# A sort's opening in a graph-network kernel: digit staircases from the integers, both image halves ahead of the columns, all tiles normalised on ScalarE

## The reference

```python
h = jnp.maximum(_layernorm(x, axis=-1), 0.0)                  # x: 1024 x 512
h = (h - mean_over_nodes) * rsqrt(var_over_nodes + EPS) * bn_w + bn_b
# graph convolution over 16384 edges (src, dst) and 1024 loops
deg = segment_sum(ones, dst);  norm = deg[src]**-0.5 * deg[dst]**-0.5
h = segment_sum((h @ W)[src] * norm[:, None], dst) + b
for i in range(4):      # four layers: attention against cond, then a gated feed-forward
    ...
h = graph_convolution(h) ; return x + h + x_in
```

## Time and profile before

| | us |
|---|---|
| median of 3 runs | 2408.67 (2406.61 to 2410.69) |
| the profiled execution, its own time | 2408.46 |
| its span, first to last instruction | 2406.7 |
| mean granted TensorE clock | 0.994 |

### The profile page before, as it was taken

One profiled execution on the slowest core, in us unless ns is written; L12 is line 12 of the kernel. 1 busy time (PEld: TensorE's weight loads), 2 busy tenths in 40 slices (PEclk: granted clock), 3 DMA queues, 4 the chain that ended last, 5 costly groups with the idle time before them and its releaser, 6 DMA issues.

```text
span 2406.7 us, 32703 instructions
## 1 busy us (share of the span) xinstructions
PE 2357.1 (98%) x11951; PEld 1956.0 (81%) x11951; DVE 1651.5 (69%) x3177; ACT 1119.3 (47%) x2206; POOL 669.1 (28%) x439
## 2 busy tenths in 40 slices
PE   6899999999999999999999999999999999999999
PEld 4358888888888888878888888878888888888887
DVE  9986767775566767775666767775566766775554
ACT  9954444644334444644334444644334444554332
POOL 3111000066540000066540000066540000066540
PEclk9999999999999999999999999999999999999999
DMA  2031000122211100122211110122211100122222
GB/s 79 19 127 40 36 33 21 36 69 76 66 58 36 36 34 20 36 69 76 67 57 36 36 35 19 36 64 77 65 62 36 36 21 33 36 66 75 67 102 86
DMA packets 83306, 124.99 MB, mean 52 GB/s; under 512 B 5904, under 2 KB 63888, under 8 KB 78288
## 3 DMA queue, kind: packets, MB, share of 16 engines
q1 hardware_dynamic: 82864, 118.75, 14.9%
q10 hardware_dynamic: 288, 4.19, 0.4%
HBM read 116.36 MB, written 6.55 MB: 51 GB/s over the span
## 4 chain that ended last, share of the span: by engine, by line
PE 88%; DVE 8%; ACT 3%; issue 1%; POOL 0%; DMA 0%; SPq 0%; DVEq 0%; ACTq 0%; POOLq 0%
PE ps L2026 19%; PE ps L2028 19%; PE ps L2027 19%; PE ps L2365 7%; PE ps L2369 7%; PE ps L2367 6%; PE ps L2273 2%; PE ps L2290 2%; PE ps L2292 2%; DVE oh_d L1504 1%; PE ps L2287 1%; PE ps L2563 1%; DVE w_lo L1889 1%; DVE z L1884 1%; ACT z L1024 1%
## 5 line engine op out<-in xcount | busy, mean ns | idle before, releaser
L623 POOL TENSOR_TENSOR rstd<-veps,mhalf 128x1 f32<-128x1 f32 x48 | 28.9, 602 | 892.9 <-DVE veps L1294 892.9
L724 POOL TENSOR_TENSOR f_lo<-ff,f_hi 128x512 fp32r<-128x512 f32 x128 | 167.0, 1315 | 165.4 <-ACT f_hi L1183 165.3
L1957 DVE TENSOR_TENSOR h<-h,ps 128x512 f32<-128x512 f32 x256 | 168.9, 684 | 63.1 <-PE ps L2028 62.5
L975 ACT ACTIVATE v_hi<-ps 128x512 fp32r<-128x512 f32 x128 | 76.8, 600 | 285.0 <-PE ps L2028 285.0
L2026 PE MATMUL ps<-cond_hi,w_hi 128*128 128x512 f32 x512 | 202.1, 395 | 0.0
L2026 PE MATMUL ps<-wf_hi,f_hi 128*128 128x512 f32 x512 | 199.6, 390 | 2.0 <-DVE ff L1941 2.0
L2026 PE MATMUL ps<-w_hi,cond_hi 128*128 128x512 f32 x512 | 200.8, 392 | 0.0
L2028 PE MATMUL ps<-w_hi,cond_lo 128*128 128x512 f32 x512 | 200.3, 391 | 0.0
L2027 PE MATMUL ps<-cond_lo,w_hi 128*128 128x512 f32 x512 | 200.1, 391 | 0.0
L2028 PE MATMUL ps<-cond_hi,w_lo 128*128 128x512 f32 x512 | 200.1, 391 | 0.0
L2027 PE MATMUL ps<-w_lo,cond_hi 128*128 128x512 f32 x512 | 199.9, 390 | 0.0
(11 more groups left out here) (327 smaller groups left out, 6430.3 us busy)
## 6 DMA issues: line engine op xcount, KB each, us to landing
stage<-in_pieces SPq DMA_DIRECT2D x82, 512.0 KB, 3.3
stage<-in_condT SPq DMA_DIRECT2D x31, 1024.0 KB, 4.8
stage<-in_pieces SPq DMA_DIRECT2D x224, 128.0 KB, 2.6
at_s<-at_hi ACTq DMA_DIRECT2D x2, 2048.0 KB, 8.2
at_hi<-at_s SPq DMA_DIRECT2D x4, 1024.0 KB, 6.5
x<-in_x SPq DMA_DIRECT2D x2, 1024.0 KB, 6.9
out<-h SPq DMA_DIRECT2D x8, 256.0 KB, 2.0
bias_row<-in_rows SPq DMA_DIRECT2D x6, 256.0 KB, 3.9
```

Source lines behind the costliest of these rows:

```text
L724: pool.tensor_tensor(f_lo[q % 2][:, c, half * HALF:(half + 1) * HALF], ff[:, s % 2, :], bits(f_hi[q % 2][:, c, half * HALF:(half + 1) * HA ...
L1957: dve.tensor_tensor(h[:, t, :], h[:, t, :], ps[:, down_bank(q, t), :], ALU.add)\
```

## The change

Line numbers of the code after are given as such. The change touches the opening only.

- Digit staircases. ScalarE's 32 signs read the integer destination `ends_i` with steps of 32 in place of the shifted, converted digit. VectorE makes the first 9 itself, as 0 or 2, right ahead of `x_stats_of(0)`; ScalarE makes 8 at its start, 9 after `need_row`, 6 after the first eight column signs. The shift and half of the cast are gone, and one small instruction is added ahead of `deg`.
- `x_stats_of(1)` moves on VectorE from behind the positions to before them; `z1` of tiles 4 to 7 moves from VectorE to ScalarE; TensorE transposes all eight tiles before column 0; `pos` and `chunk_up` stand in bank 3 instead of 7.
- `d_low` on GpSimd is split in halves, one ahead of the normalisation constants and one behind.
- On ScalarE `w_high` of both pieces moves from before `z1` to behind the signs and digits; on GpSimd `w_low` moves with it.
- On VectorE the scatters 8 to 15 move from before `batch_scale` to behind it; on ScalarE signs 8 to 15 move from before `y` to behind it. The block of products on TensorE moves from column 15 to column 7, and each later product four columns earlier.

The numbers and places:

```diff
-    G_AT = {G_FIRST + 1 + 9 * n // 2: one for n, one in enumerate(G_GROUPS)}
+    G_AT = {G_FIRST - 3 + 9 * n // 2: one for n, one in enumerate(G_GROUPS)}
-        pos, chunk_up = ps[:, 7, 0:CHUNKS], ps[:, 7, CHUNKS:2 * CHUNKS]
+        pos, chunk_up = ps[:, 3, 0:CHUNKS], ps[:, 3, CHUNKS:2 * CHUNKS]
```

On GpSimd:

```diff
+            d_low_of(0)
             for half in range(2):
...
-                if half == 0:
-                    w_low(0, 0, attn_place(0, 0, 0), attn_place(1, 0, 0))
+            d_low_of(1)
+            w_low(0, 0, attn_place(0, 0, 0), attn_place(1, 0, 0))
             pool.wait_ge(b_ln, 2 * KC)
```

On ScalarE:

```diff
+            act.wait_ge(ends_in, 32)
+            act.wait_ge(steps_ok, 1)
+            d_apart(APART_BY_VECTOR, APART_BY_VECTOR + 8)
             act.wait_ge(col_mm, 1)
...
-            for n in range(2):
-                w_high(n, n, attn_place(0, 0, n))
             for t in range(4):
                 z1_of(t)
+            for t in range(4):
+                x0T_of(t)
+            for t in range(4, NT):
+                z1_of(t)
+            for t in range(4, NT):
+                x0T_of(t)
             act.wait_ge(iota_ok, 1)
             act.wait_ge(pos_ok, 4)
             signs(0, 8)
-            for t in range(4):
-                x0T_of(t)
-            for t in range(4, NT):
-                x0T_of(t)
-            d_apart(18, 32)
-            signs(8, G_FIRST + 1)
+            d_apart(26, 32)
+            for n in range(2):
+                w_high(n, n, attn_place(0, 0, n))
             for k in range(KC):
```

On VectorE:

```diff
+            for v in range(APART_BY_VECTOR):
+                last = dve.tensor_scalar(d_high[:, v, :], ends_i[:, 1, :], 32.0 * v, 2.0, ALU.is_ge, ALU.mult)
...
             x_stats_of(0)
+            x_stats_of(1)
...
-            x_stats_of(1)
+            batch_stats(0)
+            low_equal()
+            batch_stats(1)
             dve.wait_ge(pay_ok, 3)
             dve.wait_ge(pos_ok, 5)
             scatters(0, 8)
-            for t in range(4, NT):
-                z1_by_vector(t)
-            low_equal()
-            batch_stats(0)
-            batch_stats(1)
-            scatters(8, G_FIRST + 1)
             batch_scale()
             for k in range(2):
                 y_of(k)
+            scatters(8, 10)
...
+            scatters(10, 13)
             y_low(2)
...
+            scatters(13, G_FIRST + 1)
             y_low(3)
```

On TensorE:

```diff
-                if c == G_FIRST:
+                if c == 7:
                     pe.wait_ge(w_ok, 1)
```

More of the change, by code:

```diff
@@ L610, in _ @@
                       allow_small_or_imprecise_dtypes=True).then_inc(iota_ok, 1)
-            pool.iota(steps[:, :], pattern=[[-2, 32]], base=1, channel_multiplier=0,
+            pool.iota(steps[:, :], pattern=[[-64, 32]], base=1, channel_multiplier=0,
                       allow_small_or_imprecise_dtypes=True).then_inc(steps_ok, 1)
@@ L632, in _, with d_low_of @@
             pool.wait_ge(iota_ok, 1)
-            pool.tensor_tensor(d_low[:, :, :], d5[:, 0, :].unsqueeze(2).broadcast_to([P, CHUNKS, 32]),
-                               iota0[:, 0:32].unsqueeze(1).broadcast_to([P, CHUNKS, 32]),
-                               ALU.subtract).then_inc(d_low_ok, 1)
+            def d_low_of(which):
+                r, n = slice(which * CHUNKS // 2, (which + 1) * CHUNKS // 2), CHUNKS // 2
+                pool.tensor_tensor(d_low[:, r, :], d5[:, r].unsqueeze(2).broadcast_to([P, n, 32]),
+                                   iota0[:, 0:32].unsqueeze(1).broadcast_to([P, n, 32]),
+                                   ALU.subtract).then_inc(d_low_ok, 1)
+            d_low_of(0)
             for half in range(2):
@@ L802, in cond_high, with d_apart @@
                                ACT.Copy).then_inc(c_hi, 1)
+            def d_apart(first, end):
+                for v in range(first, end):
+                    last = act.activation(d_high[:, v, :], ends_i[:, 1, :], ACT.Sign, scale=2.0, bias=steps[:, v:v + 1])
+                last.then_inc(d_apart_ok, 1)
+            act.wait_ge(ends_in, 32)
+            act.wait_ge(steps_ok, 1)
+            d_apart(APART_BY_VECTOR, APART_BY_VECTOR + 8)
             act.wait_ge(col_mm, 1)
@@ L820, in _ @@
                 .then_inc(need_ok, 1)
[L822 to L829, removed]
+            d_apart(APART_BY_VECTOR + 8, 26)
             def z1_of(t):
-                act.wait_ge(x_rs, 4)
+                act.wait_ge(x_rs, 4 + t // 4 * 4)
                 act.activation(z1[:, t, :], x1[:, t, :], ACT.Identity, scale=x_rstd[:, t:t + 1],
@@ L885, in _ @@
                 y_high(k)
-            at = G_FIRST + 1
+            at = 8
             for t in range(NT):
@@ L1320, in _ @@
             dve.tensor_scalar(lane_of, iota1[:, 0:P], P + 0.5, None, ALU.subtract).then_inc(pay_ok, 1)
+            for v in range(APART_BY_VECTOR):
+                last = dve.tensor_scalar(d_high[:, v, :], ends_i[:, 1, :], 32.0 * v, 2.0, ALU.is_ge, ALU.mult)
+            last.then_inc(d_far_ok, 1)
             def x_stats_of(half):
@@ L2071, in g_product @@
                     last.then_inc(g_mm, 1)
-            for t in range(4):
-                if t == 3:
-                    pe.wait_ge(pos_ok, 5)
+            for t in range(NT):
                 x_transpose(t)
@@ L2087, in _ @@
                 if c == 7:
-                    for t in range(4, NT):
-                        x_transpose(t)
                     pe.wait_ge(d_oh_ok, 1)
-                    pe.wait_ge(d_apart_ok, 2)
+                    pe.wait_ge(d_far_ok, 1)
+                    pe.wait_ge(d_apart_ok, 3)
                     for e in range(0, CHUNKS, 4):
```

35 lines of the change are left out of this document (16 added, 19 removed).

## The result

The changed kernel took 2411.38 us (median of 20 runs, 2408.83 to 2413.63) against 2406.99 us for the kernel before, timed beside it on the same chip (20 runs, 2406.05 to 2410.69). The ratio is 1.0017 with an interval from 1.0011 to 1.0023, so it is about 4 us slower, and under the 0.2% named above.

What follows compares the result with a forecast made beforehand. VectorE was taken as the bound, ScalarE a hair behind. Column-loop delay after idle and last-sign allowances, 3.4 us, added to the profiled 2408.46 gave 2411.9 us; range 2410.5 to 2413.5, with rivals and run spread 2407.8 to 2415.2.

Steps and rivals of the forecast that it cites:

- The mechanism: Opening: batch constants queue behind late `w_low` on GpSimd, holding `bn` to 31.1; moved work and lost clock add 3.4 us.
- Half clock: TensorE's block of products: after some 4 us idle, 9 to 10 products run at 1.2 GHz, costing 1.9 us more.
- The loop: Column loop: ScalarE's 4.8 us delay at sign 24 shrinks by 0.9 idle and 0.5 last-sign lead to 3.4.
- First half of `d_low`: GpSimd, ahead of the normalisation constants: half of 7.23 us, over by 8.8 us.
- The trace does not bear it out: Rejected the rule that GpSimd and two-port VectorE instructions exclude each other, since `dinv` for 2.76 us left scatters unslowed.
- The rival that the gain arrives: Batch constants not held, y 3.5 us earlier: 2407.1 us, if VectorE's wait before `bn` is under about 2; chance 0.08.

Runs made afterwards that it cites:

- e1: Changed kernel with GpSimd's batch constants ahead of `w_low` instead of behind it; 2408.37 us, ratio 1.0008 to the kernel before.
- e2: Changed kernel with scatters and signs 8 to 15 ahead of `bn` again and TensorE's block of products back behind column 15; 2408.4 us, ratio 1.0005 to before.
- e3: Changed kernel with 14 extra, unread matmuls on TensorE between the digits and the block of products; 2411.33 us, ratio 1.0016 to before.
- e9: Changed kernel with eight extra, overwritten matmuls on TensorE before the aggregate; 2409.71 us in one run.
- e4: Changed kernel with VectorE's nine digit staircases made twice, the second set into memory that nothing reads; 2411.27 us in one run.
- e2a: Changed kernel with scatters and signs 8 to 15 ahead of `bn` again, TensorE's block left behind column 7; 2411.23 us in one run.
- e10: Kernel before the change with eight extra, overwritten matmuls on TensorE ahead of the aggregate; 2406.17 us, ratio 0.9995 to before.
- e5: As e1, with the second weight piece's `w_low` also on GpSimd instead of VectorE; 2411.25 us, ratio 1.0015 to before.
- e6: As e1, but the first `w_low` made by VectorE behind its y parts instead of by GpSimd; 2407.0 us, ratio 0.9998 to before.
- e8: As e6, with eight extra, overwritten matmuls on TensorE before the aggregate; 2405.13 us, ratio 0.9995 to before.
- e11: The kernel of e8 run again beside e10 on the same chip; 2407.08 us, ratio 0.9999 to before.
- e7: As e6, with one digit staircase on VectorE instead of nine and the other 31 on ScalarE; 2408.71 us, ratio 1.0009 to before.

## Why the prediction was right

**The mechanism held step by step.** Forecast and row: `w_high` 27.3 and 27.6 (where `w_lo` is released), `w_lo` over at 29.7 and 30.0, `bn` 31.1 and 31.48, VectorE idle 3.9 and 4.06, ScalarE 3.5 and 3.58, block 35.05 and 35.40, fold over at 40.5 and 40.4, `stairs` late by 1.1 and 0.83, sign 16 at 43.3 and 43.56, column 16 at 3.3 and 3.37 us later. e1 shows that GpSimd's queue held `bn`, e2 that the column work put behind the wait, together with the block put ahead of it, costs as much, e3 that the clock's share is 1.2 to 2.1 us.

**The time, 2411.9, is 0.5 over the median, and part of that is luck.** The delay was put at 3.4 us and is 4.4 by the medians (2411.38 less 2406.99) and 4.9 at the first layer's mark; the time it was added to, 2408.46, had a wait in a later layer that makes its stretch behind the mark 2.2 us longer than after's, and the median of before, 2406.99, suggests that most executions do without it. The two errors stand against each other.

**Terms that were off.**
- Half clock. Foreseen were 4 us of it and 1.9 us lost, against 3.1 us (35.4 to 38.5) and 1.5 in this profile. In e9, where the same stretch is unaltered, the block took 5.28 us, 2.4 more than at full clock. So 1.5 and 2.4 are two drawings of one term, and 1.9 lies between them.
- The loop. Forecast was that ScalarE's 4.8 us shrink to 3.4 by 0.9 of idle time and by 0.5 that its last sign was ahead. The 0.9 were there. But the last sign was ahead of the last scatter's end by 0.5 again (`xs_hi`, right behind the last sign, at 79.07; the last scatter from 79.21 for 0.33), so those 0.5 were no reserve. ScalarE became the bound, busy for 35.61 of the 36 us from 44 to 80 where VectorE is for 35.41, and VectorE lost 0.4 in the loop in pauses too short for a row. With the 3.37 of column 16 that makes 3.75.
- First half of `d_low`: 8.8 us foreseen, 10.15 by its row. It cost nothing since `x_veps` had to wait for VectorE until 10.4 in any case; e4 shows that of 1.2 us more 0.9 reach z1.
- The clock at the aggregate was not in the sum: 0.8 us more lost there than before (below).

**The step that failed** is "The trace does not bear it out". I had looked in the earlier trace rows for a VectorE instruction made longer by `dinv`, and the scatters were not. But `dinv` did not stand for all GpSimd work: beside `w_lo` one scatter was held (e2). And the other side stood in the same row: `dinv` itself. It takes 2.76 us in before and 1.64 after, and all fourteen profiles fall into two groups. Where VectorE's y subtraction started 0.04 to 0.05 us ahead of it (before, e2, e2a, e10) it took 2.67 to 2.76; where the subtraction started 0.7 us behind it (the other ten), 1.64 or 1.65, and the subtraction its normal 1.22. The difference is that subtraction's 1.1 us. The subtraction in before, and in after:

```profile
39.12 1.23 DVE L1430 TENSOR_TENSOR w_lo<-x,w_hi 128x1024 fp32r<-128x1024 f32 x1
```

```profile
42.49 1.22 DVE L1436 TENSOR_TENSOR w_lo<-x,w_hi 128x1024 fp32r<-128x1024 f32 x1
```

With e1, e5, e2 and e4 the runs show it in both directions: VectorE's 128x4 instruction held for 2.1 us, its y parts for 2.0, a scatter for 2.2, GpSimd's `d_low` stretched by 1.4 and 2.6; and in e6, where GpSimd is silent from 27 to 37 us, nothing is held there. So the engines do not meet only at semaphores. The Trainium skill, page SBUF — State Buffer, section Who interferes with whom, says more than I took from it: a VectorE instruction in a two-port mode, or one with two inputs in SBUF beside a GpSimd instruction that reads SBUF, shares a pair of ports with GpSimd, and the one that is issued first has it until its end. The runs agree for each instruction just named, though no row tells which of them is in a two-port mode. They do not agree for the ten profiles in which `dinv` came first: in after it runs from 41.77 to 43.41, and the subtraction, with two inputs in SBUF, starts at 42.49 and takes 1.22 us, where the rule would hold it until 43.41. The measurement decides here; why this GpSimd instruction of 128x8 holds nothing was not tried.

That the forecast held nevertheless is shown by the rows: the staircases on VectorE were not the side that was held (5.38, 1.30 us, statistics at 7.45), what they did to GpSimd ended at 10.15, ahead of 10.4, and `w_low` fell into VectorE's idle time. It cost the first repair (e1) 2 us and e5 its whole gain.

**The rival that the gain arrives** named VectorE's wait before `bn` as its point. e6 comes nearest to what it would have given: 75.80, so 0.45 us earlier than before, not 1.4. With `bn` at 27.4 VectorE has no idle time until the loop, so the 1.1 us of `w_lo`, which it must do there, count in full; that they are the missing 1 us is argued and not measured.

**Where the whole time departs from the opening.** With the clock granted in full, the aggregate takes 43.7 us to the mark in every kernel that has it (e1, e3, e8 to e11); before lost 0.9 there, after 1.7. With 0.3 between the decoding and the aggregate, 3.75 has become 4.9 at the mark. Behind the mark, before's profile has a wait that is longer than any of after's (the chain that ended last, 1590 to 1612 us of before):

```profile
1595.58 2.80 POOL w_lo L628
...
1600.75 4.68 DMA stage<-in_pieces
```

The load of one weight piece held the chain there. Such a wait came in one layer of after as well (2.70 us from 522.68), in three layers of e3. Its place and length change between executions; what decides them was not tried. The difference of the two waits, 2.0 us, is nearly all of the 2.2 us that the single profiles give back (2408.46 to 2411.14 is 2.7), while the medians keep 4.4.

## What to carry to other kernels

Work that is moved ahead of a wait can be worth nothing until each in-order queue that feeds the wait has been read for what stands in front of the awaited instruction; here one line on GpSimd's queue hid 3 us of gain. When such a line is moved, look at what runs on VectorE beside its new place, and time both instructions, the one that may be held and the one that may be stretched. And when an idle stretch of TensorE grows, price the clock of what follows it, and keep columns or other useful work in the stretch rather than ahead of it.

## What the runs showed of the hardware

- A GpSimd `tensor_tensor` of 128x1024 (2.39 us) held a VectorE `tensor_tensor` of 128x4 until it was over (2.31 instead of 0.16 us, e1), and one VectorE `tensor_scalar` of 128x128 (2.51 us, e2). A GpSimd `tensor_tensor` of 128x8 (`dinv`, 1.64 us) held neither kind: a VectorE subtraction that started 0.7 us behind it took its normal 1.22. Where the subtraction started 0.04 us ahead, `dinv` took 2.76.
- The same pause does not always cost the same clock. Before the aggregate TensorE idled 3.39 us in before, after, e1 to e7 and e2a (3.38 in two of them). Behind the pause the granted clock stayed at 1.00 in e1 and e3; it was 0.50 from 143 to 146 in before and from 142 to 146 in e6. Before the block, pauses of 0.2 to 2.94 us kept it and those of 3.98 to 4.88 us lost it. What tells the 3.39 us pauses apart stays open.
